# The first attention of an eight-layer block: scores over every key, or over nine gathered keys and a mean key

## The reference

```
kv_c = kv @ W_kvc ; q_c = q @ W_dq                  # 128 and 192 latent columns
q_nope, q_rope = q_c @ W_uq, rope(q_c @ W_qr)       # 16 heads x 128, 16 heads x 64
k_nope, k_rope = kv_c @ W_uk, rope(kv_c @ W_kr)     # one rotary key for all heads
scores = (q_nope . k_nope + q_rope . k_rope) / sqrt(192)
good = (k_ids <= seg) & (k_ids >= seg - 8)          # seg: one integer of 0..255 for a query
scores = where(good, scores, -1e30)
out = softmax(scores) @ (kv_c @ W_uv) ; return out @ W_o
```

## Time and profile before

| | |
|---|---|
| median of 3 runs | 2430.27 us (2427.51 to 2432.77) |
| the profiled execution, first to last instruction | 2431.7 us; its time outside this span is not shown |
| mean granted TensorE clock | 0.975 of 2.4 GHz |
| first attention, end of its layernorm to start of the next | 24 to 530.6 us |
| moved by DMA | 263.7 MB |

### The profile page before, as it was taken

One profiled execution on the slowest core, in us unless ns is written; L12 is line 12 of the kernel. 1 busy time (PEld: TensorE's weight loads), 2 busy tenths in 40 slices (PEclk: granted clock), 3 DMA queues, 4 the chain that ended last, 5 costly groups with the idle time before them and its releaser, 6 DMA issues. The chain is left out here.

```text
span 2431.7 us, 33068 instructions
## 1 busy us (share of the span) xinstructions
PE 2274.3 (94%) x9625; PEld 1365.2 (56%) x9626; DVE 978.5 (40%) x2530; ACT 712.2 (29%) x1675; POOL 372.5 (15%) x513
## 2 busy tenths in 40 slices
PE   7899999998898899998999999699999999899999
PEld 4454444444665566666455655255565655345688
DVE  5645455544333433335612223872222222521276
ACT  2444453540111466666111110211111111051131
POOL 6100000000222100000011113501111110700052
PEclk9999999998999999999999999899999999899999
DMA  9401010013775000001445554152444452551130
GB/s 343 133 1 36 0 36 0 0 56 101 255 241 164 31 10 14 14 14 37 146 147 192 198 196 159 40 173 88 147 160 136 160 165 73 174 210 64 62 126 36
DMA packets 170065, 263.72 MB, mean 108 GB/s; under 512 B 13230, under 2 KB 106798, under 8 KB 169469
## 3 DMA queue, kind: packets, MB, share of 16 engines
q1 hardware_dynamic: 139965, 186.06, 23.3%
q0 software_dynamic: 15040, 49.30, 6.7%
q10 hardware_dynamic: 14976, 27.27, 3.0%
HBM read 212.78 MB, written 49.81 MB: 108 GB/s over the span
## 5 line engine op out<-in xcount | busy, mean ns | idle before, releaser
L1368 PE MATMUL bank<-f2r_wd,f2b_hT 128*128 (+1 forms) x300 | 137.2, 593 | 1.4 <-DVE f2b_hT L1479 1.4
L1349 PE MATMUL bank<-f2r_wg,f2b_xT 128*128 x400 | 129.2, 467 | 2.0 <-issue 2.0
L1349 PE MATMUL bank<-f2r_wu,f2b_xT 128*128 x400 | 126.7, 460 | 0.0
L1466 DVE TENSOR_TENSOR f2b_h<-bank,f2b_acted 128x352 f32<-128x352 f32 x50 | 26.2, 524 | 202.8 <-PE bank L1349 202.8
L1812 PE MATMUL bank<-l0a_vo,l0a_zT 128*128 128x512 f32 x224 | 101.5, 596 | 3.2 <-DVE l0a_zT L1977 3.2
L1349 PEld LDWEIGHTS bank<-f2r_wu,f2b_xT 128*128 128x128 f32 x400 | 76.3, 191 | 42.7 <-issue 0.7
L1876 ACT ACTIVATE l0a_p<-l0a_p,l0a_low 112x375 f32<-112x375 f32 x128 | 77.2, 607 | 77.5 <-DVE l0a_low L1968 76.4
L1958 DVE CUSTOM_DVE_ANT_0 l0a_p<-bank,xn 112x375 f32<-112x375 f32 x128 | 70.2, 549 | 67.5 <-PE bank L1784 35.7
L1782 PE MATMUL bank<-l_kvcT,xnT 128*112 128x375 f32 x256 | 92.3, 482 | 5.0 <-ACT xnT L1905 5.0
L2153 PEld LDWEIGHTS bank<-l1w_v,ctxT 128*125 128x125 f32 x768 | 88.7, 188 | 8.4 <-issue 0.6
L1349 PEld LDWEIGHTS bank<-f2r_wg,f2b_xT 128*128 128x128 f32 x400 | 73.1, 193 | 35.1 <-issue 4.0
(11 more groups left out here) (418 smaller groups left out, 4346.2 us busy)
## 6 DMA issues: line engine op xcount, KB each, us to landing
slot_rows<-zeros SPq DMA_DIRECT2D x2, 7424.0 KB, 37.8
slot_rows<-f2b_y ACTq DMA_DIRECT2D x50, 256.0 KB, 3.4
f1r_wg<-in_l_wg SPq DMA_DIRECT2D x16, 704.0 KB, 4.2
f1r_wu<-in_l_wu SPq DMA_DIRECT2D x16, 704.0 KB, 5.6
f2r_wg<-in_l_wg SPq DMA_DIRECT2D x16, 704.0 KB, 4.3
f2r_wu<-in_l_wu SPq DMA_DIRECT2D x16, 704.0 KB, 5.7
xn<-in_l_w_ffn SPq DMA_DIRECT2D x12, 768.0 KB, 4.4
f0r_wg<-in_l_wg SPq DMA_DIRECT2D x16, 512.0 KB, 5.0
```

The source lines that it names most:

```text
L1349: mm = pe.matmul(bank[:, 0:width], xT[:, v, k, :], w[:, bass.ds(at, 1), k, :].rearrange("p o f -> p (o f)"), start=(k == 0), stop=(k == KD ...
L1368: mm = pe.matmul(bank_y[v][:, :], hT[0:fn, v, c, :], wd[0:fn, bass.ds(at, 1), c, :].rearrange("p o f -> p (o f)"), start=(c == 0), stop=(c ...
L1466: dve.tensor_tensor(h[:, v, :], up, acted[:, v, :], ALU.mult).then_inc(h_done, 1)
```

## The change

Both attention stages become one. The key stage still goes sample by sample, but stores for every key one row of 256 values in device memory (`kv_rows`): its latent and, twice, its rotary part, rows and not columns. Row 375 is the mean key. A sample's 112 queries are split into 8 groups of 2 by 7. For every 7 queries, 63 rows (9 keys each) and the mean row are gathered: POOL makes the indices and issues 8 indirect DMAs per sample, each of 128 rows, into one of three windows; the third window lies over `w_uq` and waits for the weight products. PE turns the windows (`turn_latents`, `turn_rotary`), and the scores of 7 queries in 16 heads (112 rows) stand against 64 columns. All 16 heads are done at once, so there is one pass over the samples, and the products of the weights are made once. The mask (112 x 16 x 64 for a sample) keeps, for each query, its own nine columns; POOL makes it, in one buffer. The queries are made in four quarters, two samples each, in steps 1, 3 and 5 after the first. The output weights' products are made in step 2; their inputs lie over `ctxT`, so they load after the sums, the clear of `slot_rows` comes behind them, and the router stage loads `ctxT` again behind its first expert weights. Two of the eight shares of the decayed sums come after the first rotations.

The diff, cut to its core:

```diff
-def latent_project_stage(nc, s, d, a, w):
 def latent_attention_stage(nc, s, d, a):
+        def _(sp):                                # sync
+            a.load_products(sp, d)
+            for b in range(B):
+                ...
+                sp.dma_start(s.kv_rows[b].rearrange("(t p) n -> p t n", p=128),
+                             rows[:, b % 2, :, :]).then_inc(rows_stored[b % 2], 16)
+            sp.wait_ge(kv_done, B)
+            sp.wait_ge(sums.summed, KD * B)
+            a.load_output(sp, d)
+            clear_scratch(sp, s)
+        def _(pool):                              # gpsimd
+            def make_mask(b):
+                if b:
+                    pool.wait_ge(s_masked, 2 * b)
+                pool.tensor_tensor(mask[:, :, :], a.key_shifts[:, :].unsqueeze(1).to_broadcast([HQ, 2 * VG, KEYS]),
+                                   each(query_ids[:, of_b]), ALU.add).then_inc(mask_step, 1)
+                ...
+                pool.tensor_tensor(mask[:, :, :], mask[:, :, :], mask[:, :, :], ALU.mult).then_inc(mask_step, 1)
+                ...
+                pool.tensor_scalar(mask[:, :, :], mask[:, :, :], float(((T - 1) // 2) ** 2), None, ALU.is_gt)\
+                    .then_inc(mask_step, 1)
+                ...
+                pool.tensor_copy(mask[:, :, KEYS - 1], mean_masked[:, of_b]).then_inc(mask_made, 1)
+            def gather(b):
+                pool.wait_ge(rows_stored[b % 2], 16 * (b // 2 + 1))
+                if b >= WINS:                     # WINS = 3
+                    pool.wait_ge(z_done, 2 * (b - WINS + 1))
+                if b == WINS - 1:
+                    pool.wait_ge(qk_done, 1)
+                for i in range(VG):               # VG = 8
+                    g = b * VG + i
+                    pool.indirect_dma_start(wins[b % WINS][:, i, :], None, s.kv_rows[b], ...)
+            make_mask(0)
+            for b in range(WINS):
+                gather(b)
+            for b in range(1, B):
+                make_mask(b)
+                if b + WINS - 1 < B:
+                    gather(b + WINS - 1)
+        def _(pe):                                # tensor, after the key stage
+            def scores(n):                        # waits: kwl_copied, kwr_copied, lat_copied, rope_added, s_masked
+                ...
+                        pe.matmul(s.bank[v][0:HQ, i * KEYS:(i + 1) * KEYS],
+                                  qT[:, 2 * VG * v + group_of(n, i), :, :].rearrange("p h q -> p (h q)"),
+                                  kwL[:, i, v * KEYS:(v + 1) * KEYS], start=(i == 0), stop=False)
+                ...
+            def project(m):
+                pe.wait_ge(z_copied, 2 * min(m + 2, B))
+                ...
+                k = queries_in(m + 3)
+                if k is not None:
+                    pe.wait_ge(rope_mul, 20 * (k + 1))
+                for j in range(H):
+                    mm = pe.matmul(s.bank[7][:, :], zT[:, m % 2, j, 0:P], vo[:, j, :], start=(j == 0), stop=(j == H - 1))
+            ...
+            for n in range(STEPS):                # B + 2
+                if n < B:
+                    scores(n)
+                if 1 <= n <= B:
+                    turn(n - 1)
+                if queries_in(n) is not None:     # n in (1, 3, 5)
+                    for r in range(2):
+                        rotary_queries(queries_in(n), r)
+                        queries(queries_in(n), r)
+                if n == 2:
+                    output_weights()
+                if 0 <= n - 3 < TILES:
+                    project(n - 3)
+                if n + 1 < B:
+                    turn_latents(n + 1)
+                if 1 <= n <= B:
+                    mix(n - 1, 0)
+                if n + 1 < B:
+                    turn_rotary(n + 1)
+                if 1 <= n <= B:
+                    mix(n - 1, 1)
+        def _(act):                               # scalar: per step pT copy, exp, query copies, vo copies, window copies
+                if n < B:
+                    act.wait_ge(shifted, n + 1)
+                    act.activation(own(n), own(n), ACT.Exp, scale=SCALE0).then_inc(e_done, 1)
+                ...
+                if n == 2:
+                    for j in range(H):
+                        act.wait_ge(vo_done, j + 1)
+                        act.activation(vo[:, j, :], s.bank[6 + j % 2][:, :], ACT.Copy).then_inc(vo_copied, 1)
+                if n + 1 < B:
+                    copy_latents(n + 1)
+                    copy_rotary(n + 1)
+        def _(dve):                               # vector
+            def shift(n):
+                dve.wait_ge(mask_made, n + 1)
+                dve.wait_ge(s_done, n + 1)
+                ...
+                for v in range(2):
+                    dve.scalar_tensor_tensor(out=p[:, n % 2, :, v, :], in0=mask[:, VG * v:VG * (v + 1), :], scalar=-MASKED,
+                                             in1=s.bank[v][0:HQ, :].rearrange("p (g n) -> p g n", g=VG),
+                                             op0=ALU.mult, op1=ALU.add).then_inc(s_masked, 1)
+                ...
+                then(dve.tensor_reduce(top[:, :], own(n), AX_X, ALU.max))
+                dve.tensor_tensor(own(n), own(n), each(top[:, :]), ALU.subtract).then_inc(shifted, 1)
+            ...
+            for n in range(B + 2):
+                if n < B:
+                    shift(n)
+                if queries_in(n) is not None:
+                    rotate(queries_in(n), 0)
+                if n < B:
+                    divide(n)
+                if queries_in(n) is not None:
+                    rotate(queries_in(n), 1)
+                if 0 <= n - 3 < TILES:
+                    add(n - 3)
+                if 1 <= n <= B:
+                    copy_mix(n - 1, 0)
+                    copy_mix(n - 1, 1)
 def router_stage(..., context=None):
             ring.load_first(sp)
+            if context is not None:
+                for k in range(KD):
+                    sp.dma_start(s.ctxT[:, k, :], context[:, k, :]).then_inc(s.ctx_reloaded, 16)
```

More of the change, by code:

```diff
@@ L1578, in sum @@
                                      accum_out=s.ctx_sums[:, k, b:b + 1]).then_inc(self.summed, 1)
-class ProjectWeights:
+class Latent:
     def __init__(self, nc, ctx, s):
[L1585 to L1600, removed]
@@ L1666, in _, with copy_queries @@
         @block.scalar
         def _(act):
+            def copy_queries(k, r):
+                for j in range(4):
+                    hp = 4 * r + 2 * (j // 2)
+                    act.wait_ge(lat_done, 8 * k + 4 * r + j + 1)
+                    to = qT.rearrange("p g (hp two) q -> p hp two g q", two=2)[:, hp:hp + 2, j % 2, :, :]
+                    act.activation(to, s.bank[2 + j][:, 0:8 * VG * QN].rearrange("p (s g q) -> p s g q", s=2, q=QN), ACT.Copy)\
+                       .then_inc(lat_copied, 1)
@@ new lines, in divide, with copy_mix @@
+            def divide(n):
+                dve.wait_ge(e_done, n + 1)
+                then(dve.tensor_reduce(total[:, :], own(n), AX_X, ALU.add))
+                then(dve.reciprocal(inv[:, :], total[:, :]))
+                dve.tensor_tensor(own(n), own(n), each(inv[:, :]), ALU.mult).then_inc(p_done, 1)
+            def copy_mix(b, half):
+                banks = (4, 5) if half else (6, 7)
+                dve.wait_ge(z_done, 2 * b + half + 1)
+                if b >= 2 and not half:
+                    dve.wait_ge(y_done, b - 1)
+                if b == 0 and not half:
+                    for i in range(2):
+                        dve.wait_ge(rows_stored[i], 16 * B // 2)
+                for v in range(2):
+                    mixed = s.bank[banks[v]][:, 0:VG // 2 * HQ].rearrange("p (g h q) -> p g h q", h=H, q=QN)
+                    for t, g0, g1, q0, q1, at in pieces_of(b, half, v):
+                        n = g1 - g0
+                        to = zT[:, t % 2, :, at - q0:at - q0 + 2 * QN * n] if at >= q0 else None
+                        if n == 1:
+                            op = dve.tensor_copy(zT[:, t % 2, :, at:at + q1 - q0], mixed[:, g0, :, q0:q1])
+                        else:
+                            to = to.rearrange("p h (g q) -> p g h q", q=2 * QN)[:, :, :, q0:q1]
+                            op = dve.tensor_copy(to, mixed[:, g0:g1, :, q0:q1])
+                op.then_inc(z_copied, 1)
@@ new lines, in _ @@
+            for b in range(B + 1):
+                if b < B:
+                    mean(b)
+                if b:
+                    rotate_keys(b - 1)
+                if b < B - 2:
+                    sums.sum(dve, b, B)
+            rotate(0, 0)
+            rotate(0, 1)
+            for i in range(B - 2, B):
+                sums.sum(dve, i, B)
+            for n in range(B + 2):
[5 more added lines that the diff above has]
+                    divide(n)
+                if queries_in(n) is not None:
+                    rotate(queries_in(n), 1)
[4 more added lines that the diff above has]
+                    copy_mix(n - 1, 1)
```

(19 more changed lines are left out.)

851 lines of the change are left out of this document (465 added, 386 removed).

## The result

| | before | after |
|---|---|---|
| median | 2430.38 us (4 runs beside it) | 2326.20 us (2325.67 to 2327.62, 4 runs) |
| ratio, 95% interval | | 0.9574, 0.9560 to 0.9588 |
| next layernorm starts | 530.59 | 425.65 |
| from there to the end of the span | 1901.1 | 1899.1 |
| profiled execution: time, span | span 2431.7 | 2326.55, 2324.7 |

A forecast was written before the change was run, and what follows sets the result against it. PE's columns bound the first attention. Walking the new order (start to 119, then steps) gave 413, plus 12 for clock drops: layernorm at 425 instead of 530.6, so 2430.3 - 105.6 = 2325, own range 2300 to 2345, 8 in 10 2270 to 2375.

The forecast's parts named there:

- PE work: -155 by the sum: First attention: 259 us of PE work removed, 88 added for samples and 16 for rotary queries, net -155 us.
- The key stage: end at 76: Start of the first attention: key stage stays bound by DVE and ends at 76 instead of 73 (73 to 80).
- the four decayed sums (0.71 and more each) stay: Key stage on DVE: four decayed sums, 0.71 us and more each, stay in six of the eight samples.
- Steps 2, 3 and 5: the late mask: Attention steps: POOL's mask, behind a gather, comes 17.6 us after the start; step 2 takes 39, steps 3 and 5 57 each.
- Steps 4 and 6: 25 forecast: Attention steps without query making: 25 us each, the mask at 17.6 just hidden because the output product covers it.
- The clock: 12 forecast: First attention: PE stands still in some seven places, each losing 1.7 us to a lower clock, 12 in all.
- Rival 3: First attention: frequent waits keep PE at 1.2 GHz and the kernel gets slower, 2466 with 60% of work slow; chance 0.06.
- rival 2: Attention steps: POOL is dear, mask passes 4.3 to 5.8 us, 7 more in each of steps 2 to 6: 2360; chance 0.16.
- Rival 1: Attention steps: POOL is in time or the mask is not the wait, step 2 28, steps 3 and 5 45: 2285; chance 0.25.
- the floor of 2275: Whole kernel: the time if all 155 us of PE work were saved, 2275.
- The rule weighed: POOL against DVE reading two SBUF tiles: they exclude each other; masks of steps 2 to 6 free, otherwise 8 us more.
- Moved transfers: Later clear, output-weight loads and context reload: no cost taken; reload up to 18 us, slow gather landing a few us once.

The follow-up runs named there:

- e5_pool_busy: Changed kernel with the first pass of POOL's first mask done 16 times more, beside DVE's decayed sums: 2340.90 us, 14.7 more.
- e1_order: Changed kernel with only POOL's order altered, each mask made ahead of the gather that waits for a window: 2272.08 us, 54.1 less.
- e7_all: e6_windows plus the output weights' copies ahead of sample 2's exponential and the output product in bank 6: 2255.91 us, ratio to before 0.9278.
- e6_windows: e1_order with ACT's two copies of window 1 ahead of the exponential of sample 0: 2261.96 us, 10.1 less than e1_order.
- e3_copies: Changed kernel with ACT's 16 copies of the output weights ahead of the exponential of sample 2: 2311.03 us, 15.2 less.
- e4_rotate_first: Changed kernel with DVE's rotations ahead of the shift and ACT's query copies ahead of the exponential: 2300.70 us, 25.5 less.

## Why the prediction was right

**PE work: -155 by the sum.** At nearly the full clock it is 304.7 - 480.1 = -175. The prices of the small products were too high: a sample's scores took 5.05 (to 191.33 in step 3) where I took 6.1, and the rotary products of half a quarter of the queries 3.4, so 27 in all where I took 37: 8 and 10 of the 20 us. The clock then took the 20 back. So the measured -156 meets the forecast by luck.

**The key stage: end at 76, measured 66.4.** The step that failed is "the four decayed sums (0.71 and more each) stay": that row's 712 ns is a mean. In the changed kernel, and in the kernel before, the view of that line shows (shortest, median, longest in ns):

```profile
L2292 DVE CUSTOM_DVE_ANT_0 xn<-ctxT,xn x32: 540/544/547, 40.6 to 94.9; 128x375 f32<-128x375 f32 x32
```

```profile
L1576 DVE CUSTOM_DVE_ANT_0 l2s_weighted<-ctxT,l2s_coef x32: 536/544/1350, 32.6 to 70.5; 128x375 f32<-128x375 f32 x32
```

The long ones lay beside POOL's work on the old mask (not every sum beside it was long), which the change removed; `e5_pool_busy` brings long sums back. So I kept a cost whose cause I had seen in the earlier trace rows and had put to the wrong side, as a price for the masks. This explains 24 x 0.168 = 4.0 of the 9.6 us. For the other 5.6 no step can be named, as the 76 was put and not summed. One part that the trace shows is the start: the first mean began at 39.99, where before the first rotation of keys began at 42.40, and I had counted the wait for the first context copy as a loss. The times behind it were early by somewhat more (first scores 93.97 for 105.5, second 106.50 for 119).

**Steps 2, 3 and 5: the late mask.** Forecast 17.6 us after the step's start; in step 3 it was 203.88 - 186.28 = 17.60, from gathers of 9.9 and a mask of 7.0. The gathers begin 0.7 behind the step's start, and the mask is 0.6 cheaper than forecast: the mechanism is the forecast one, the exact number luck. Steps 3 and 5 took 58.6 and 58.1 for 57, step 2 43.0 for 39, since 28 of the output weights' instructions took 15.84, in part at half the clock:

```profile
149.11 1.90 PE L1967 MATMUL bank<-ctxT 128*128 128x512 f32 x4
166.31 15.84 PE L1967 MATMUL bank<-ctxT 128*128 128x512 f32 x28 [15.31 <-ACT ctxT L2078]
```

**Steps 4 and 6: 25 forecast, 31.1 and 32.5 measured.** The failed step is "the mask at 17.6 is just hidden, since the output product covers it". It covers the mask, not what follows it: the mix waits for the bank that DVE's addition of the output product (L2182) frees, and DVE reaches that addition only behind shift and division. Timelines of DVE and PE in step 4:

```profile
262.42 1.28 DVE L2147 SCALAR_TENSOR_TENSOR xn<-l0a_mask,bank 112x512 f32<-112x512 f32 x2 [16.45 <-POOL l0a_mask L1769]
...
270.03 0.74 DVE L2182 SCALAR_TENSOR_TENSOR x<-bank,tanh_g,x 128x512 f32<-128x512 f32 x1
```

```profile
264.40 1.04 PE L1895 MATMUL bank<-ident,l_w_uq 128*128 128x128 f32 x8
270.87 2.05 PE L1957 MATMUL bank<-xn,l0a_win 64*128 64x112 f32 x16 [5.43 <-issue]
```

**The clock: 12 forecast, about 20 measured**, in these waits and in those not foreseen. A drop can cost more than the 1.7 that I took for each: in step 3 the four groups behind the waits for the rotation took 1.76, 1.76, 3.25 and 5.24, where they take 0.99, 0.99, 1.75 and 3.29 in step 1, 5.0 us more. Rival 3 is out: no stretch was below 0.80.

**The sum** came out at 425.65 for 425 only because the errors cancel: start -12.5; step 1 +5.8, step 2 +4.0, steps 3 and 5 +2.7, steps 4 and 6 +13.6, the rest -1.0 (59.0 for 60), and those steps hold the clock that I had as 12 beside them: +0.6. What was right is the late mask and what it does to steps 2, 3 and 5; that the number is right to 1 us is luck.

**Rivals.** The mask's passes took 1.9, 1.9 and 2.8 for 2.55 each, so rival 2 is out. Rival 1 was false of this kernel, yet `e1_order` is the kernel in which it holds: 2272 for 2285. That it and `e7_all` lie below the floor of 2275 shows the size of the PE term, not a mechanism: with 175 in place of 155 the floor is 2255.

**The rule weighed.** The masks of samples 2 to 6 were free of DVE, as forecast: their passes took 1.9, 1.9 and 2.8 each time. In samples 1 and 7, whose masks had time, the second pass lay beside DVE's subtraction L2152, which reads two tiles in SBUF. In sample 1:

```profile
101.70 1.78 DVE L2152 TENSOR_TENSOR xn<-xn,l0a_top 112x1024 f32<-112x1024 f32 x1
102.48 2.75 POOL L1764 TENSOR_TENSOR l0a_mask<-l0a_mask 112x1024 f32<-112x1024 f32 x1
```

Elsewhere they take 1.22 and 1.89. Here both lost, 0.56 and 0.86. That in `e5_pool_busy` nearly all of the cost fell on DVE may come from the passes standing one right behind the other; it wasn't tried.

**Moved transfers.** From the layernorm on the time lies between 1892.9 and 1901.3 us in the changed kernel and its variants, at 1901.1 before, so no cost of the context's reload is seen; that it has 18 us of room wasn't tried. The gather of step 2 landed in time beside the clear: PE turned that window at 181.99 with no wait.

## What to carry to other kernels

When a change takes work from the engine that bounds a stage, walk the new order on every other engine: an instruction that needs only ids, queued behind one that waits for a buffer, can delay all that is queued behind its users. Follow a wait past the addition that frees the bank, not only to its first cover. And read the median and the longest beside a mean: two lengths of one instruction can come from two neighbours, and the change may remove one of them.

## What the runs showed of the hardware

- A wait of PE can cost more than itself, and need not. Shortening a wait by 4.4 us gave 10.1 (`e6_windows`); 51 us more idle time in the change came with 20 more in clock. But `e3_copies` and `e4_rotate_first` have 15 and 25 us less idle time than the changed kernel, and PE is busy for no less than its 324.2 us. Their first attentions, each as one stretch:

```profile
29.50:414.06 384.56, 327.77 (x2201) 234.02 (x2199) 174.74 (x338) 70.82 (x110) 116.54 (x95) 0.89 0.29 91
```

```profile
29.50:401.26 371.76, 324.65 (x2200) 230.63 (x2198) 176.00 (x338) 70.71 (x110) 116.62 (x95) 0.91 0.30 93
```

  Nor is the drop tied to one wait: behind the same gaps of 1.34 and 1.20 us the scores of sample 0 took 3.33 and 1.79 in the changed kernel, and in `e7_all` a part of them ran slow:

```profile
94.23 4.69 PE L1923 MATMUL bank<-l0a_kwL,xnT 128*112 128x64 f32 x32 [1.20 <-issue]
98.85 3.25 PE L1928 MATMUL bank<-l0a_kwR,l0a_qrT 64*112 64x64 f32 x32
```

  What decides there stays open.
- On POOL a comparison with a constant (L1766) took 2.77 for 1024 columns, an addition or a square 1.9: fewer inputs were not cheaper. The earlier trace rows had hinted at it, had not.
- The issue of a gather took 0.95 on POOL, and 1.09 to 1.24 in eight of the sixteen cases between 47 and 68 us. Most of these lay beside DVE's sums; what lengthens an issue wasn't tried.
